# Cross attention of a perceiver block: value tiles taken in three blocks per pair, and the 65 left-over context positions spread over the four row quadrants

## The chip, the cores and the metric

The kernel runs on one core of a Trainium2 chip. The metric is the device time of one execution in microseconds; before and after are compared by the median of several runs.

## The reference, cut to what matters

Thirty-two sequences of 64 positions (width 512) pass through a cross attention to a context of 1601 positions each, then a causal self attention, then a mixture of experts. The change touches the cross attention alone:

```python
def _L0_xattn_ref(input_seq, condition_seq, Wq, bq, Wk, bk, Wv, bv):
    q = jnp.einsum('bsd,ed->bse', input_seq, Wq) + bq
    k = jnp.einsum('btd,ed->bte', condition_seq, Wk) + bk
    v = jnp.einsum('btd,ed->bte', condition_seq, Wv) + bv
    scores = jnp.einsum('bse,bte->bst', q, k)
    attn = jax.nn.softmax(scores, axis=-1)
    attended = jnp.einsum('bst,bte->bse', attn, v)
    return attended

x = x + _L0_xattn_ref(_layernorm(x, axis=-1), ctx_1024, ...)   # ctx: (32, 1601, 512)
```

All of it is float32. The kernel folds the key weights into the queries and applies the value weights after the attention, so that the context itself serves as keys and as values.

## The kernel before, in words

`prepare` (L155) computes the folded queries of all sequences and stores them to the tensor `q_n`, and loads the first context pieces. `cross` (L404) is the cross attention. Then come `self_attention` (L622) and `mixture`, which the change leaves alone.

`cross` works on 16 pairs of sequences. The two sequences of a pair sit in the two column halves of the TensorE array (64 columns each). A sequence's 1601 context positions are 12 full tiles of 128 positions and one rest of 65 (`FULL` = 12, `REST` = 65, `TILES` = 13). They lie in SBUF in slots: the first slot of a pair holds tiles 0 to 6, the second tiles 7 to 11 and the rest (index 5 of the slot, partitions 0 to 64). There are five slots (`SLOTS`), so a pair and a half is in flight beyond the one that is read.

For one pair the score part has 32 steps (`STEPS_S`), 16 on each slot. A step is one transpose on VectorE (`blocks`, L470 to L477: 32x32 blocks of 32 context columns into the ring `z` of 8 entries) and eight matmuls on TensorE (`score`, L554 to L566): one for each row quadrant of 32 rows and each column half. Row quadrant `tb` takes the positions that lie in partitions 32 tb to 32 tb + 31 of each tile. The widths are in `WIDTH` (L416): each quadrant streams 224 columns in the first 16 steps; in the last 16, quadrants 0 and 1 stream 192 columns (five full tiles and 32 of the rest), quadrant 2 streams 161 and quadrant 3 streams 160.

Then VectorE takes the maxima (`greatest`, L479), ScalarE the exponentials (L533 to L536, in five `PIECES`, each with a running sum), TensorE turns the probabilities (`transpose_prob`, L568, 13 transposes in four groups, each copied out by ScalarE, L544 and L547), and TensorE multiplies them by the values (`attend`, L579 to L589: one call for a tile, with two matmuls of 128 rows by 64 columns and 512 streamed columns). The result is scaled, turned (`transpose_attended`, L591) and stored. Each float32 matmul of `score` and `attend` stands in the profile as two matmul records and two weight loads, so a score step has 16 matmul records and an `attend` has 4.

These parts are interleaved by hand in the TensorE stream (L599 to L619), which is unrolled over all pairs: while pair p is scored, the probabilities of pair p-1 are turned ahead of steps 0, 1, 3 and 5, seven value tiles are taken one at a time ahead of steps 9, 12, 15, 18, 21, 24 and 27, and the other six after step 31. The exponentials of pair p read the score banks, so step 0 of pair p+1 waits for them (L602); the six last tiles run meanwhile.

SyncE (L434 to L464) stores results, loads queries and loads the next context pieces: the first slot of a pair is reloaded when seven value tiles are done (`s_pv`, L451), the second when all thirteen are (L454). ScalarE's copy of a turned result (L525) waits for the store two pairs earlier.

Of the kernel before, what the change touches and what calls it, by code (L numbers as in the profile page):

```python
# [38 lines left out]
D1, F1 = 32, 64  # L39
FULL = CTX // P  # L40
REST = CTX - FULL * P
TILES = FULL + 1
MASKED = -3.0e38


def apart(e, spare):


    e.sem_inc(spare[e.engine], 1)


def tile_rows(j):
    return P if j < FULL else REST


def program(nc, a, out):
# [98 lines left out]
def prepare(nc, sem, area, ps, a, ident, qa, qbias, halves, slots, qs, s_c, s_qs, s_qd):  # L155
# [23 lines left out]
    with nc.Block() as block:  # L179
# [44 lines left out]
        @block.vector  # L224
        def _(vec):
            S.start(vec, "dve")

            def normalise(i, u):
                n = i * 2 + u
                vec.wait_ge(s_x[u], i * 16 + 16)  # L230
                layer_norm_stats(vec, stats, mv, xt[u], S, "stat", "mv", n)
                past(vec, "rstd", n + 1)
                past(vec, "mv", n + 1)
                past(vec, "t", n - 1)
                for par in range(2):
                    vec.tensor_scalar(xn[u][:, par * D:(par + 1) * D], xt[u][:, par * D:(par + 1) * D],
                                      mv[:, par, 0:1], rstd[:, par:par + 1], ALU.subtract, ALU.mult)\
                       .then_inc(S["xn"], 1)

            def row_biases(n):  # L240
                past(vec, "r", n + 1)
                vec.tensor_tensor(qbias[:, bass.ds(n * 2, 2)], ps[:, RB, 16:18],
                                  cols[:, 2 * DC:2 * DC + 1].to_broadcast([P, 2]), ALU.add).then_inc(S["re"], 1)
            vec.memset(slots[slot_of(1)][64:P, :, 5, :], 0.0).then_inc(S["pad"], 1)
            normalise(0, 0)
            vec.wait_ge(s_b, 32)
            for c in range(DC):
                vec.tensor_copy(bq_wide[:, c, :], bqc[:, c:c + 1].to_broadcast([P, P])).then_inc(S["wide"], 1)
            for m in range(DC):
                past(vec, "fuse", m + 1)  # L250
                vec.tensor_copy(wqk[:, m, :], ps[:, m, :]).then_inc(S["fused"], 1)
            past(vec, "col", 1)
            vec.tensor_copy(cols, ps[:, RB, 0:2 * DC + 1]).then_inc(S["cold"], 1)
            past(vec, "cold", 1)
            normalise(0, 1)
            with vec.Fori(0, QUADS // 2 - 1) as i:
                for u in range(2):
                    row_biases(i * 2 + u)
                    normalise(i + 1, u)
            for u in range(2):  # L260
                row_biases(QUADS - 2 + u)
# [91 lines left out]
def slot_of(k):  # L353
    return (k + 3) % SLOTS


def context_landed(k):

    return sum(32 if j % 2 == 0 else 64 for j in range(k % SLOTS, k + 1, SLOTS))


def load_context(sp, a, slots, s_c, k, seqs=(0, 1)):

    pair, g = divmod(k, 2)
    u = slot_of(k)
    for b in seqs:
        seq = pair * 2 + b
        main = a["ctx"][seq, 0:FULL * P, :].rearrange("(p j) d -> p j d", j=FULL)
        if g == 0:
            sp.dma_start(slots[u][:, b, 0:7, :], main[:, 0:7, :]).then_inc(s_c[u], 16)  # L370
        else:
            sp.dma_start(slots[u][:, b, 0:5, :], main[:, 7:FULL, :]).then_inc(s_c[u], 16)
            sp.dma_start(slots[u][0:REST, b, 5, :], a["ctx"][seq, FULL * P:CTX, :]).then_inc(s_c[u], 16)


def load_queries(sp, a, qs, s_qs, p):
# [27 lines left out]
def cross(nc, sem, zone, ps, a, ident, qbias, slots, qs, s_c, s_qs, s_qd, early):  # L404
# [5 lines left out]
    probt = zone(TILES, P)  # L410
    att = zone(D)
    att_t = zone(DC, P)
    mx, sums = zone(4), zone(5)
    top, bias = zone(1), zone(1)
    total, recip = zone(1), zone(1)
    WIDTH = (416, 416, 385, 384)  # L416
    PIECES = ((0, 0, TILES, 32), (1, 0, TILES, 32), (2, 0, FULL, 32), (3, 0, FULL, 32), (2, FULL, TILES, 1))
    EXPS = len(PIECES)
    TB, OB, AB = 4, 6, 7

    s_pad = sem("cr_pad")
# [10 lines left out]
    with nc.Block() as block:  # L432
# [33 lines left out]
        @block.vector  # L466
        def _(vec):
            def blocks(p, n):
                g, db = divmod(n, 16)
                k, at = 2 * p + g, STEPS_S * p + n  # L470
                nt = GTILES[g]
                if db == 0:
                    vec.wait_ge(s_c[slot_of(k)], context_landed(k))
                if at >= RING:
                    vec.wait_ge(s_s, at - RING + 1)
                vec.transpose(z[:, at % RING, :, 0:nt * 32].rearrange("p b (j t) -> p b j t", t=32),  # L476
                              slots[slot_of(k)][:, :, 0:nt, db * 32:(db + 1) * 32]).then_inc(s_z, 1)  # L477

            def greatest(p):  # L479
                vec.wait_ge(s_s, STEPS_S * (p + 1))  # L480
                for tb in range(4):
                    vec.reduce_max(mx[:, tb:tb + 1], ps[:, tb, 0:WIDTH[tb]], AX.X).then_inc(s_mx, 1)
                vec.wait_ge(s_mx, 4 * p + 4)
                vec.tensor_reduce(top, mx, AX.X, ALU.max, negate=True).then_inc(s_top, 1)
                vec.wait_ge(s_top, p + 1)
                if p:
                    vec.wait_ge(s_exp, EXPS * p)
                vec.tensor_scalar(bias, top, qbias[:, p:p + 1], qbias[:, p:p + 1],  # L488
                                  ALU.subtract, ALU.add).then_inc(s_bias, 1)

            def denominator(p):
                vec.wait_ge(s_exp, EXPS * (p + 1))
                vec.reduce_sum(total, sums, AX.X).then_inc(s_tot, 1)
                vec.wait_ge(s_tot, p + 1)
                if p:
                    vec.wait_ge(s_att, p)
                vec.reciprocal(recip, total).then_inc(s_rec, 1)

            vec.memset(slots[slot_of(3)][64:P, :, 5, :], 0.0).then_inc(s_pad, 1)
            vec.wait_ge(s_qd, 64 * 16)  # L500
            vec.memset(prob[:, FULL, 2, :], 0.0).then_inc(s_pad, 1)
            for p in range(PAIRS):
                for n in range(STEPS_S):
                    blocks(p, n)
                    if p and n == 1:
                        greatest(p - 1)
                    if p and n == 12:
                        denominator(p - 1)
            greatest(PAIRS - 1)
            denominator(PAIRS - 1)  # L510

        @block.scalar
        def _(act):
# [14 lines left out]
            for p in range(PAIRS):  # L528
                act.wait_ge(s_bias, p + 1)
                if p:  # L530
                    act.wait_ge(s_tot, p)
                    act.wait_ge(s_pt, 4 * p)
                for n, (tb, j0, j1, w) in enumerate(PIECES):  # L533
                    act.activation(prob[:, j0:j1, tb, 0:w],  # L534
                                   ps[:, tb, j0 * 32:(j1 - 1) * 32 + w].rearrange("p (j t) -> p j t", t=w), ACT.Exp,
                                   bias=bias[:, 0:1], accum_out=sums[:, n:n + 1]).then_inc(s_exp, 1)  # L536
                if p:
                    attended(p - 1)
                for g in range(4):
                    act.wait_ge(s_pt, 4 * p + g + 1)  # L540
                    if p and g == 0:
                        act.wait_ge(s_pv, TILES * p)
                    if g < 3:
                        act.copy(probt[:, 4 * g:4 * g + 4, :], ps[:, TB + g % 2, :].rearrange("p (j n) -> p j n", j=4))\  # L544
                           .then_inc(s_pte, 1)
                    else:
                        act.copy(probt[0:96, FULL, :], ps[0:96, TB + 1, 0:P]).then_inc(s_pte, 1)  # L547
                if p:
                    attended_out(p - 1)
            attended(PAIRS - 1)  # L550
# [3 lines left out]
        def _(pe):  # L554
# [13 lines left out]
            def transpose_prob(p, g):  # L568
# [3 lines left out]
                if n >= 2:  # L572
                    pe.wait_ge(s_pte, n - 1)
                for j in quarter(g):
                    tbs, at = (4, (j - 4 * g) * P) if j < FULL else (3, 0)
                    last = pe.transpose(ps[0:tbs * 32, TB + g % 2, at:at + P], prob[:, j, 0:tbs, :].rearrange("p b t -> p (b t)"), ident)
                last.then_inc(s_pt, 1)

            def attend(p, j):  # L579
                if j % 4 == 0:  # L580
                    pe.wait_ge(s_pte, 4 * p + j // 4 + 1)
                if j == 0 and p:
                    pe.wait_ge(s_att, p)
                r = tile_rows(j)
                slot, jj = (slots[slot_of(2 * p)], j) if j < 7 else (slots[slot_of(2 * p + 1)], j - 7)
                for b in range(2):
                    last = pe.matmul(ps[b * SEQ:(b + 1) * SEQ, OB, :], probt[0:r, j, b * SEQ:(b + 1) * SEQ],  # L587
                                     slot[0:r, b, jj, :], start=j == 0, stop=j == TILES - 1)
                last.then_inc(s_pv, 1)  # L589

            def transpose_attended(p):  # L591
# [7 lines left out]
            for p in range(PAIRS):  # L599
# [3 lines left out]
                for n in range(STEPS_S):  # L603
                    if p and n in (0, 1, 3, 5):
                        transpose_prob(p - 1, (0, 1, 3, 5).index(n))
                    if p >= 2 and n == 6:
                        transpose_attended(p - 2)
                    if p and n >= 9 and (n - 9) % 3 == 0 and (n - 9) // 3 < 7:
                        attend(p - 1, (n - 9) // 3)
                    score(p, n)  # L610
                if p:
                    for j in range(7, TILES):
                        attend(p - 1, j)
            for g in range(4):
                transpose_prob(PAIRS - 1, g)
# [1222 lines left out]
```

## Time and profile before

| what | value |
|---|---|
| median of 3 runs | 1514.75 us (1506.93 to 1524.37) |
| profiled execution, its own time | 1523.18 us |
| profiled execution, its span | 1521.4 us |
| mean granted TensorE clock | 0.935 of full speed |
| TensorE busy | 1350.5 us, 89% |
| VectorE busy | 823.1 us, 54% |
| ScalarE busy | 438.3 us, 29% |
| cross attention, first score step to last transpose | about 134.7 to 639 us of the span |

The rows below and the durations come from the profiled execution; its own time is 1.8 us above its span (what lies around the span) and 8.4 us above the median of the runs.

### The profile page before, as it was taken

What the parts mean: (1) busy time and instruction counts of PE and PEld (TensorE: products, weight loads), DVE (VectorE), ACT (ScalarE), POOL (GpSimd) and SP (SyncE); (2) the same over time, 40 slices, a digit from 0 to 9 for tenths busy, and PEclk for the clock granted to TensorE, in tenths of its full rate; (3) what the DMA queues carried; (4) which work ended last, traced back from release to release, by engine and by line L of the source; (5) the groups of instructions that cost most, each with busy time, mean ns of one, the idle gap of its engine ahead of it and who ended that gap; (6) DMA issues with size and microseconds to landing.
All of it is one profiled execution on the core that took longest, in us unless ns stands there. A gap on an engine that the chain in (4) does not pass through costs nothing.

```text
span 1521.4 us, 70167 instructions
## 1 busy us (share of the span) xinstructions
PE 1350.5 (89%) x32072; PEld 932.3 (61%) x32072; DVE 823.1 (54%) x1519; ACT 438.3 (29%) x879; POOL 208.2 (14%) x361
## 2 busy tenths in 40 slices
PE   7896799999999999889999999967888988798896
PEld 4895444444544454356666666646777876687785
DVE  1224566666665665145566555633647465347656
ACT  0230121112211221111122222203636455336544
POOL 0000000000000000001111111102424424023212
PEclk9798899999999999999999999968999999959968
DMA  5476187867886789251100111130203012532202
GB/s 194 143 219 217 38 281 273 269 210 278 300 254 213 279 291 285 72 106 56 51 28 31 55 55 42 56 84 30 111 28 139 38 73 105 222 146 87 107 28 83
DMA packets 57228, 211.96 MB, mean 139 GB/s; under 512 B 11760, under 2 KB 28144, under 8 KB 42640
## 3 DMA queue, kind: packets, MB, share of 16 engines
q1 hardware_dynamic: 57104, 210.14, 40.5%
q8 instruction: 98, 1.61, 0.4%
q14 instruction: 26, 0.21, 0.0%
HBM read 172.37 MB, written 37.75 MB: 138 GB/s over the span
## 4 chain that ended last, share of the span: by engine, by line
PE 42%; DVE 6%; issue 5%; ACT 2%; POOL 2%; DMA 1%; SPq 0%; DVEq 0%; POOLq 0%; ACTq 0%
PE ps L895 8%; PE ps L1675 5%; PE ps L1629 4%; PE ps L886 4%; PE ps L996 4%; PE ps L1644 3%; PE ps L1661 2%; PE ps L1718 2%; PE ps L1600 2%; PE ps L916 2%; PE ps L1701 2%; PE ps L1591 1%; PE ps L906 1%; DMA arena<-h_n 1%; PE ps L938 1%
## 5 line engine op out<-in xcount | busy, mean ns | idle before, releaser
L476 DVE STREAM_TRANSPOSE arena<-arena 128x384 f32<-128x384 f32 (+1 forms) x512 | 275.6, 586 | 133.2 <-PE ps L563 132.7
L563 PE MATMUL ps<-arena 32*64 32x224 f32 (+3 forms) x8192 | 241.3, 348 | 30.3 <-issue 22.0
L563 PEld LDWEIGHTS ps<-arena 32*64 32x64 f32 x8192 | 160.6, 134 | 140.9 <-DVE arena L476 85.8
L587 PE MATMUL ps<-arena 128*64 128x512 f32 (+1 forms) x832 | 207.1, 609 | 0.6 <-issue 0.6
L895 PE MATMUL ps<-arena 128*128 128x256 f32 x512 | 116.3, 386 | 6.2 <-ACT arena L847 6.2
L1515 ACT COPY arena<-ps 128x512 f32<-128x512 f32 x128 | 75.1, 587 | 149.8 <-PE ps L1644 79.4
L895 PEld LDWEIGHTS ps<-arena 128*128 128x128 f32 x512 | 97.1, 192 | 21.7 <-ACT arena L847 7.2
L534 ACT ACTIVATE arena<-ps,arena 128x416 f32<-128x416 f32 (+2 forms) x80 | 41.1, 530 | 229.1 <-DVE arena L488 229.1
L587 PEld LDWEIGHTS ps<-arena 128*64 128x64 f32 (+1 forms) x832 | 49.3, 136 | 86.7 <-issue 86.7
L1675 PE MATMUL ps<-arena 64*64 64x32 f32 x4096 | 91.6, 245 | 10.6 <-DVE arena L1352 5.7
L1675 PEld LDWEIGHTS ps<-arena 64*64 64x64 f32 x4096 | 85.8, 164 | 16.0 <-issue 12.5
L1335 DVE SCALAR_TENSOR_TENSOR arena<-ps,arena 128x512 f32<-128x512 f32 x64 | 68.7, 1104 | 42.6 <-PE ps L1661 42.3
L1629 PE MATMUL ps<-arena 64*32 64x128 f32 x4096 | 71.1, 277 | 14.9 <-issue 6.5
L1629 PEld LDWEIGHTS ps<-arena 64*32 64x32 f32 x4096 | 59.5, 107 | 26.5 <-issue 22.9
L721 POOL MEMSET arena<- 128x128 f32 x1 | 0.2, 205 | 537.3 <-POOLq L432 537.3
L886 PE MATMUL ps<-arena 128*128 128x512 f32 x128 | 61.7, 618 | 8.2 <-ACT arena L876 4.8
L1701 PE MATMUL ps<-arena 64*64 64x256 f32 x1024 | 63.4, 401 | 6.0 <-DVE arena L1345 3.5
L1644 PE MATMUL ps<-arena 32*32 32x64 f32 x4096 | 56.7, 232 | 13.0 <-issue 5.9
L1214 POOL COPY arena<-arena 128x512 f32<-128x512 f32 x64 | 42.3, 666 | 176.9 <-ACT arena L1527 94.0
L799 DVE SCALAR_TENSOR_TENSOR arena<-ps,arena 128x512 f32<-128x512 f32 x32 | 20.6, 686 | 74.1 <-PE ps L906 74.1
L1644 PEld LDWEIGHTS ps<-arena 32*32 32x32 f32 x4096 | 47.7, 108 | 21.1 <-issue 20.6
L313 PE MATMUL ps<-arena 128*128 128x256 f32 x256 | 59.5, 391 | 0.0
(135 smaller groups left out, 1879.0 us busy)
## 6 DMA issues: line engine op xcount, KB each, us to landing
arena<-ctx SPq DMA_DIRECT2D x32, 1792.0 KB
arena<-ctx SPq DMA_DIRECT2D x32, 1280.0 KB
arena<-q_n SPq DMA_DIRECT2D x64, 256.0 KB, 14.0
h_n<-arena SPq DMA_DIRECT2D x16, 1024.0 KB, 4.4
arena<-h_n SPq DMA_DIRECT2D x16, 1024.0 KB, 9.9
arena<-x SPq DMA_DIRECT2D x16, 512.0 KB, 4.6
x_n<-arena SPq DMA_DIRECT2D x16, 512.0 KB, 3.1
arena<-x_n SPq DMA_DIRECT2D x16, 512.0 KB, 3.9
```

The lines of the kernel that those rows point to most:

```text
L476: vec.transpose(z[:, at % RING, :, 0:nt * 32].rearrange("p b (j t) -> p b j t", t=32), slots[slot_of(k)][:, :, 0:nt, db * 32:(db + 1) * 32 ...
L563: last = pe.matmul(ps[b * SEQ:(b + 1) * SEQ, tb, g * 224:g * 224 + w], qs[p % 2][r, db, b * SEQ:(b + 1) * SEQ], z[r, at % RING, b, 0:w], s ...
L587: last = pe.matmul(ps[b * SEQ:(b + 1) * SEQ, OB, :], probt[0:r, j, b * SEQ:(b + 1) * SEQ], slot[0:r, b, jj, :], start=j == 0, stop=j == TI ...
L886: x = pe.matmul(ps[:, par, :], ats[:, c, par::2], w["xwv"][:, c, :], start=c == 0, stop=c == DC - 1)
L895: last = pe.matmul(ps[:, bank, m % 2 * QROWS:(m % 2 + 1) * QROWS], w[n][:, c, m * P:(m + 1) * P], lnt[:, c, :], start=c == 0, stop=c == DC ...
L996: last = pe.matmul(ps[:, 4 + par, :], aot[:, c, par::2], w["swo"][:, c, :], start=c == 0, stop=c == DC - 1)
L1335: vec.scalar_tensor_tensor(h[:, q, :, at].rearrange("p j g -> p g j"), ps[:, b:b + 2, :].rearrange("p b (g x) -> p (b g) x", x=2 * F1)[:, ...
L1515: act.copy(mid[u].rearrange("p (b x) -> p b x", b=2), ps[:, 2 * u:2 * u + 2, 0:256]).then_inc(s_me, 1)
L1629: last = pe.matmul(ps[c * R:(c + 1) * R, 4 * v + hf, o * P:(o + 1) * P], tab_st[v][r, o, :], x, start=True, stop=True)
L1644: last = pe.matmul(ps[q * R:(q + 1) * R, 2 * u + c // 2, m * F1:(m + 1) * F1], xs[rows_c, m, :], four(st_a[u])[rows_c, m // 2 * 2 + k, m % ...
L1675: last = pe.matmul(ps[k * F1:(k + 1) * F1, 2 * u + t, g * D1:(g + 1) * D1], st_h[u][rows_t, g * F1:(g + 1) * F1], two(st_a[u])[rows_t, k, ...
L1701: last = pe.matmul(ps[t * E:(t + 1) * E, 2 * (g % 4) + hf, o % 2 * 2 * P:(o % 2 + 1) * 2 * P], tab_dn[v][r, o, :], x, start=True, stop=True)
```

## The change

The 65 left-over positions are no longer put into partitions 0 to 64 of the last tile. Sixteen of them go to the start of each of the four row quadrants (partitions 0, 32, 64 and 96), and the 65th to partition 16. So each quadrant streams 176 or 177 columns in the last 16 steps. The load of the rest becomes five transfers for a sequence instead of one. The exponentials become four of 384 columns, one of 4 x 16 columns and one of a single column. The last tile is used with all 128 partitions, the unused ones set to zero beforehand. The value tiles of pair p-1 are taken in blocks of three ahead of steps 11 and 22, and seven after step 31.

```diff
+RQ = REST // 4
-def tile_rows(j):
-    return P if j < FULL else REST
@@ prepare, vector
-            vec.memset(slots[slot_of(1)][64:P, :, 5, :], 0.0).then_inc(S["pad"], 1)
+            vec.memset(slots[slot_of(1)][:, :, 5, :], 0.0).then_inc(S["pad"], 1)
@@ context_landed
-    return sum(32 if j % 2 == 0 else 64 for j in range(k % SLOTS, k + 1, SLOTS))
+    return sum(32 if j % 2 == 0 else 32 * 6 for j in range(k % SLOTS, k + 1, SLOTS))
+
+def rest_of(tb):
+    return ((tb * 32, RQ, FULL * P + tb * RQ),) + (((RQ, 1, CTX - 1),) if tb == 0 else ())
@@ load_context
-            sp.dma_start(slots[u][0:REST, b, 5, :], a["ctx"][seq, FULL * P:CTX, :]).then_inc(s_c[u], 16)
+            for tb in range(4):
+                for row, n, first in rest_of(tb):
+                    sp.dma_start(slots[u][row:row + n, b, 5, :], a["ctx"][seq, first:first + n, :]).then_inc(s_c[u], 16)
@@ cross
-    mx, sums = zone(4), zone(5)
+    mx, sums = zone(4), zone(6)
-    WIDTH = (416, 416, 385, 384)
-    PIECES = ((0, 0, TILES, 32), (1, 0, TILES, 32), (2, 0, FULL, 32), (3, 0, FULL, 32), (2, FULL, TILES, 1))
-    EXPS = len(PIECES)
+    RAT = FULL * 32
+    WIDTH = (RAT + RQ + 1, RAT + RQ, RAT + RQ, RAT + RQ)
+    EXPS = 6
@@ cross, vector
-            vec.memset(slots[slot_of(3)][64:P, :, 5, :], 0.0).then_inc(s_pad, 1)
+            vec.memset(slots[slot_of(3)][:, :, 5, :], 0.0).then_inc(s_pad, 1)
-            vec.memset(prob[:, FULL, 2, :], 0.0).then_inc(s_pad, 1)
+            vec.memset(prob[:, FULL, :, :], 0.0).then_inc(s_pad, 1)
@@ cross, scalar
-                for n, (tb, j0, j1, w) in enumerate(PIECES):
-                    act.activation(prob[:, j0:j1, tb, 0:w],
-                                   ps[:, tb, j0 * 32:(j1 - 1) * 32 + w].rearrange("p (j t) -> p j t", t=w), ACT.Exp,
-                                   bias=bias[:, 0:1], accum_out=sums[:, n:n + 1]).then_inc(s_exp, 1)
+                for tb in range(4):
+                    act.activation(prob[:, 0:FULL, tb, :], ps[:, tb, 0:RAT].rearrange("p (j t) -> p j t", t=32), ACT.Exp,
+                                   bias=bias[:, 0:1], accum_out=sums[:, tb:tb + 1]).then_inc(s_exp, 1)
+                act.activation(prob[:, FULL, :, 0:RQ], ps[:, 0:4, RAT:RAT + RQ], ACT.Exp,
+                               bias=bias[:, 0:1], accum_out=sums[:, 4:5]).then_inc(s_exp, 1)
+                act.activation(prob[:, FULL, 0, RQ:RQ + 1], ps[:, 0, RAT + RQ:RAT + RQ + 1], ACT.Exp,
+                               bias=bias[:, 0:1], accum_out=sums[:, 5:6]).then_inc(s_exp, 1)
-                        act.copy(probt[0:96, FULL, :], ps[0:96, TB + 1, 0:P]).then_inc(s_pte, 1)
+                        act.copy(probt[:, FULL, :], ps[:, TB + 1, 0:P]).then_inc(s_pte, 1)
@@ cross, tensor
-                    tbs, at = (4, (j - 4 * g) * P) if j < FULL else (3, 0)
-                    last = pe.transpose(ps[0:tbs * 32, TB + g % 2, at:at + P], prob[:, j, 0:tbs, :].rearrange("p b t -> p (b t)"), ident)
+                    at = (j - 4 * g) * P
+                    last = pe.transpose(ps[:, TB + g % 2, at:at + P], prob[:, j, :, :].rearrange("p b t -> p (b t)"), ident)
-                    last = pe.matmul(ps[b * SEQ:(b + 1) * SEQ, OB, :], probt[0:r, j, b * SEQ:(b + 1) * SEQ],
-                                     slot[0:r, b, jj, :], start=j == 0, stop=j == TILES - 1)
+                    last = pe.matmul(ps[b * SEQ:(b + 1) * SEQ, OB, :], probt[:, j, b * SEQ:(b + 1) * SEQ],
+                                     slot[:, b, jj, :], start=j == 0, stop=j == TILES - 1)
-                    if p and n >= 9 and (n - 9) % 3 == 0 and (n - 9) // 3 < 7:
-                        attend(p - 1, (n - 9) // 3)
+                    if p and n in (11, 22):
+                        for j in range(3):
+                            attend(p - 1, (0, 3)[n // 22] + j)
-                    for j in range(7, TILES):
+                    for j in range(6, TILES):
                         attend(p - 1, j)
```

## Rows read from the trace of the kernel before

**Rows 1.** The page, busy time of engines and the instruction queue.

```profile
PE 1350.5 (89%) x32072; PEld 932.3 (61%) x32072; DVE 823.1 (54%) x1519; ACT 438.3 (29%) x879; POOL 208.2 (14%) x361
...
q8 instruction: 98, 1.61, 0.4%
```

**Rows 2.** Windows by pair: length, busy PE, PEld, DVE, ACT, POOL; clock, DMA share, GB/s.

```profile
555.72:589.78 34.06, 30.43 (x586) 14.96 (x581) 19.78 (x40) 5.96 (x16) 0.00 (x0) 0.95 0.95 303
589.78:618.45 28.67, 28.38 (x588) 14.21 (x582) 18.50 (x38) 5.96 (x16) 0.00 (x0) 1.00 0.62 220
sum 428.70, PE 407.74 PEld 202.67 DVE 275.67 ACT 83.43 POOL 0.00; mean PE 29.12 PEld 14.48 DVE 19.69 ACT 5.96 POOL 0.00
```

**Rows 3.** Timeline of PE, two stretches of one pair: start, busy, matmul records.

```profile
257.44 0.63 PE L576 MATMUL ps<-arena 128*128 128x128 f32 x4 [0.28 <-ACT arena L534]
258.00 0.63 PE L563 MATMUL ps<-arena 32*64 32x224 f32 x16
258.56 0.66 PE L576 MATMUL ps<-arena 128*128 128x128 f32 x4
259.15 1.01 PE L563 MATMUL ps<-arena 32*64 32x224 f32 x32
260.09 0.66 PE L576 MATMUL ps<-arena 128*128 128x128 f32 x4
...
279.79 1.85 PE L563 MATMUL ps<-arena 32*64 32x192 f32 x80
281.57 5.39 PE L587 MATMUL ps<-arena 128*64 128x512 f32 x24
```

**Rows 4.** Timeline of PE, 332 to 339 us and 418 to 426 us: stalls marked issue.

```profile
332.29 0.77 PE L563 MATMUL ps<-arena 32*64 32x161 f32 x23 [0.24 <-issue]
332.98 1.08 PE L587 MATMUL ps<-arena 128*64 128x512 f32 x4
333.99 1.21 PE L563 MATMUL ps<-arena 32*64 32x192 f32 x48
335.13 1.08 PE L587 MATMUL ps<-arena 128*64 128x512 f32 x4
336.14 1.21 PE L563 MATMUL ps<-arena 32*64 32x192 f32 x48
337.27 0.64 PE L587 MATMUL ps<-arena 128*64 128x512 f32 x1
338.48 1.07 PE L587 MATMUL ps<-arena 128*64 128x512 f32 x3 [0.57 <-issue]
...
418.15 0.59 PE L563 MATMUL ps<-arena 32*64 32x224 f32 x4 [0.23 <-issue]
...
425.44 0.88 PE L563 MATMUL ps<-arena 32*64 32x192 f32 x32 [0.68 <-issue]
```

**Rows 5.** Timeline of PE after its longest stall in the steady pairs.

```profile
580.71 0.71 PE L563 MATMUL ps<-arena 32*64 32x160 f32 x3 [3.24 <-issue]
581.35 1.97 PE L587 MATMUL ps<-arena 128*64 128x512 f32 x4
583.25 1.67 PE L563 MATMUL ps<-arena 32*64 32x192 f32 x48
```

**Rows 6.** Timeline of the SP queue: issue of the context loads.

```profile
279.90 0.35 SPq L372 DMA_DIRECT2D arena<-ctx  x1
...
287.00 0.82 SPq L370 DMA_DIRECT2D arena<-ctx  x2
```

**Rows 7.** Windows of 5 us: columns as in rows 2.

```profile
300.00:305.00 5.00, 3.22 (x96) 1.74 (x88) 2.54 (x5) 0.59 (x1) 0.00 (x0) 1.00 0.73 163
305.00:310.00 5.00, 4.64 (x108) 2.27 (x107) 2.39 (x5) 0.00 (x0) 0.00 (x0) 1.00 0.01 3
```

**Rows 8.** Groups by form, 0 to 600 us: exponentials, and their last piece.

```profile
L534 ACT ACTIVATE arena<-ps,arena 128x384 f32<-128x384 f32 x30 | 17.1, 584 | 0.0
...
L534 ACT ACTIVATE arena<-ps,arena 128x1 f32<-128x1 f32 x15 | 4.1, 272 | 0.0
```

More of the change, by code:

```diff
@@ L583, in attend @@
                     pe.wait_ge(s_att, p)
-                r = tile_rows(j)
                 slot, jj = (slots[slot_of(2 * p)], j) if j < 7 else (slots[slot_of(2 * p + 1)], j - 7)
                 for b in range(2):
-                    last = pe.matmul(ps[b * SEQ:(b + 1) * SEQ, OB, :], probt[0:r, j, b * SEQ:(b + 1) * SEQ],
-                                     slot[0:r, b, jj, :], start=j == 0, stop=j == TILES - 1)
+                    last = pe.matmul(ps[b * SEQ:(b + 1) * SEQ, OB, :], probt[:, j, b * SEQ:(b + 1) * SEQ],
+                                     slot[:, b, jj, :], start=j == 0, stop=j == TILES - 1)
                 last.then_inc(s_pv, 1)
```

## The prediction, made before the changed kernel ran

> **What bounds the kernel now.** I read the page first: TensorE is busy 89% of the span, the next engine 54% [rows 1]. So I looked at the windows by pair, cut where the last six value tiles begin (I call this point T). Between T = 189.75 and T = 618.45 lie 14 pairs in 428.70 us, 30.6 us each, and VectorE is busy 19.7 us and ScalarE 6.0 us of them [rows 2]. The reader is to see that TensorE's order of work sets the pair, with some 10 us to spare on VectorE. The last pair, beside a lighter DMA (share 0.62), takes 28.67 us [rows 2]; the same instructions take 30.6 in the mean. So 428.70 - 14 x 28.67 = 27.3 us, 1.95 a pair, are something other than matmuls.
>
> The timeline of TensorE says what. It stalls with the mark "issue": it waits for no semaphore. From the stall that ends at 332.29 to the one before 338.48 I count 23+4+48+4+48+1 = 128 matmul records; with a weight load each that is 256 instructions, and the second stall falls between two records of one value tile, where nothing new is waited for [rows 4]. The instruction queue moved 98 packets, 1.61 MB, so 16.4 KB each [rows 1]: code comes in equal pieces and TensorE stalls at the seam when the next is late. From seam to seam such a piece took 338.48 - 332.29 = 6.2 us, and 425.44 - 418.15 = 7.3 us [rows 4], both beside a context transfer. That is my price of a code piece beside transfers, 6.2 to 7.3, taken as 6.7. In the pair of 28.67 us TensorE is busy 28.38, so it has no such stall; at its end a value tile, three steps, a value tile and five steps are 136 records in 1.01 + 1.14 + 1.01 + 1.78 = 4.94 us [rows 3, 4], a piece in 4.6. So beside light transfers the price is at most 4.6.
>
> The Trainium skill ("Runtime: NRT & Kernel Launch", Instruction fetch mechanics) says that engines are fed in blocks of 256 instructions, the next being fetched while one executes, and that the cost of a boundary is "mostly hidden". The trace agrees on the 256 and not on the hiding: 0.24, 0.57 and 3.24 us stand open in rows 4 and 5. If the page were right for the new order, the sum would be the first rival's, below.
>
> **The change, part by part.** First, TensorE's work with code in time.
>
> Score steps: one step alone takes 258.56 - 258.00 = 0.56, two take 260.09 - 259.15 = 0.94 [rows 3]. So a step of 224 columns is 0.38 and starting a run costs 0.18. In the second half three steps take 335.13 - 333.99 = 1.14 [rows 4] and five 281.57 - 279.79 = 1.78 [rows 3]: 0.32 a step, again 0.18 to start. The slope between 192 and 224 columns is 0.06/32 = 1.9 ns a column; the four quadrants run beside each other and the widest sets the step. From 192 to 177 that is 15 x 1.9 = 28 ns, 16 steps: -0.45 us a pair (bound from the other side: zero, if something other than width holds the step near 0.32).
>
> Value tiles: a single one takes 333.99 - 332.98 = 1.01 [rows 4]; six in a row 5.39 [rows 3], so each further one (5.39 - 1.01)/5 = 0.876, 0.13 less. Now seven singles and six: 7.07 + 5.39 = 12.46. Afterwards two threes and a seven: 2 x 2.76 + 6.27 = 11.79: -0.67. The runs of score steps that a value tile opens drop from seven to two: 5 x 0.18 = -0.90. The wait of 0.28 for the exponentials at T [rows 3] goes: TensorE arrives 0.88 later. What is late next there? The exponentials: now 416, 416, 384, 384 and 1 columns, afterwards four of 384, one of 64 and one of 1; a piece more is some 0.3 (0.272 for one column, 0.584 for 384 [rows 8]), less two narrower ones, so about +0.25. 0.88 - 0.28 = 0.60 covers it, with 0.35 left. Sum of a pair: -0.45 - 0.67 - 0.90 - 0.28 = -2.3. (Laid end to end: 28.67 becomes 26.4.)
>
> The Trainium skill ("TensorEngine Tiling (Array Packing)", on mode switching) says that changing the tiling mode drains the engine. The 0.18 and 0.13 of the rows are that drain here, 0.31 for a round trip; the sum uses the rows.
>
> What the narrower things cost: the transpose of the last tile and its copy with 128 partitions instead of 96, the values with 128 rows instead of 65: nothing, streamed columns are the same. The two memsets keep their columns a partition, the one on `prob` has 128 columns instead of 32, below 0.2 us, once. VectorE: its transposes keep their size. It has 8 entries of lead; in a run of 11 steps TensorE eats 11 in about 4 us, VectorE makes them at 0.5 to 0.6 each (19.78 us busy for 32 and the maxima [rows 2]), so it makes 7 meanwhile and the lead falls to 4 and is refilled in the 2.76 us of a block. Covered.
>
> SyncE: the second slot's load grows from 4 to 12 issues at about 0.4 us (0.35 in rows 6), +3.2 us. It starts when seven tiles are done, now T - 1.7 (279.90 against 281.57), afterwards T + 1. So issues end near T + 6, just when the next load may start (T + 6.3; now 287.00, T + 5.4). Queued behind are that load, a store and the query loads; the store is not waited for until the next T + 20, the rest not until later pairs. The context itself: 2.8 MB from T + 1 at 303 GB/s, the rate of the pair whose DMA share is 0.95 [rows 2], lands near T + 10.5; TensorE needs it at step 16, near T + 18.6. Covered by 7 us, and if the small transfers cost 3 us more, by 4.
>
> Now the code. A pair has 581 pairs of load and matmul, 4.55 pieces [rows 2]. The transfers of a pair fill 279.9 to about 303.7, 24 us, then the DMA rests (share 0.73 at 300 to 305, 0.01 at 305 to 310) [rows 6, 7]. Check on the order of now: from step 9 on there are 396 records, 3.1 pieces, in 17.2 us, about 5.5 each. The first seam is met in time, the second at 6.7, the third at about 6 (its transfer load ends), the other 1.1 at 5.5: 18.8, a stall of 1.6 against 1.95 found. Afterwards: from T to step 11 there are 221 records in 13.9 us: no stall. From there 360 records, 2.8 pieces, hold only 2.76 + 3.85 + 2.76 + 3.13 = 12.5 us of work, and the transfers, which start 2.7 us later against T, last until T + 25, beside almost all of it. Seam to seam 6.7 and 6, the other 0.8 at 4.5: 16.3. Stall 3.8. So 3.8 - 1.95 = 1.85 of the 2.3 comes back: -0.45 a pair; with 0.5 us less or more of price at each of two seams, +0.5 to -1.4. I take -0.5.
>
> Sum: 13 loaded pairs x -0.5 = -6.5. The pair before T = 189.75 and the last one have light transfers: -2.3 + 0.3 each, -4. The end has one more tile behind the scores, +0.6, and pair 1 waits the +0.25 for the exponentials. Pair 0 has no value tiles and stalls for code: 0. Together -9.6, say -10. Then the clock: after the stall of 3.24 us, the granted clock fell (0.95 in that pair), a value tile took 1.97 instead of 1.08 and three steps 1.67 instead of 1.21 [rows 2, 4, 5]: 1.35 us lost. Stalls of that length become more frequent; two in the 13 pairs: +3. I forecast -7: 1523.2 - 7 = 1516 for the profiled execution, which lies 8.4 above the median of the runs; against that median 1514.75 - 7 = 1508. Its own range is -20 to +7 (the +0.5 and -1.4 of the 13 pairs), 1495 to 1522.
>
> **The rivals.** (a) Code costs what it costs now, 1.95 a pair: 15 x -2.3 + 0.9 = -34, 1481. For it: five switches fewer are certain. Against: the pieces with no value tile in them shrink to 8 x 0.3 = 2.4 to 3 us, and seam to seam 6.2 was already the floor beside transfers.
> (b) Slower: stalls join into one of over 3.2 us in every pair, and the clock falls for a stretch each time. Stretches on pure score steps give up half of their length; with the 3.4 us over which rows 5 are slow, +1.7. If the stalls also eat the whole 2.3 saved, 13 x 1.7 = +22, 1537. It decides once a seam falls early in the run of steps 11 to 21 beside transfers, piece work 3, price 7, stall 4. For it: that arithmetic, in about every second pair. Against: matmuls right after the short stalls of rows 4 keep their durations (a value tile 1.08), and only the one of 3.24 is followed by slow ones [rows 5]; and a slow stretch partly runs in time that the next piece would cost anyway.
> (c) The context arrives late for step 16, since the load starts 2.7 us later and in 12 parts: with 4 us beyond my 7 us of slack, 13 x 4 - 10 = +42, 1557. Little speaks for it.
> (d) The step stays near 0.32 at 177 columns: beside code stalls that hides most of it, -5 instead of -7, within the forecast.
>
> **How the numbers follow.** Forecast with (d) 0.58, (a) 0.24, (b) 0.13, (c) 0.05. About 1% (15 us) is what a measurement of this kernel can tell from no change. Faster by over 1%, below 1499.6: all of (a) and a quarter of the forecast's share, 0.24 + 0.14 = 0.38. Slower by over 1%, above 1529.9: half of (b) and (c), 0.11. Within: 0.51. The range reaches to (a) and half way to (b): 1477 to 1526.
>
> **What would show it.** In the changed profile: value tiles as x12, x12, x28 of 2.8, 2.8 and 6.3 us; runs of 11 steps; pairs near 30 us, not 28; no wait for the exponentials at T; "issue" stalls of 2 to 4 us, 128 records apart, in the runs between the blocks, about doubled in sum; lower clock in several pairs. Pairs of 28 us or less with stalls as now would prove the code step wrong; a wait of VectorE for a context transfer at step 16 would prove the cover wrong; pairs over 31 us with a clock below 0.95 would be (b).

## The result and the profile after

The changed kernel takes 1528.08 us (median of 20 runs, 1520.36 to 1533.9), the kernel before 1516.01 us (20 runs): ratio 1.0083, interval 1.0059 to 1.0106, so 12 us slower. The forecast was 7 us faster and the range ended at 1526: it missed in sign and in range. The profiled execution took 1529.43 us, span 1527.6.

The page of the changed kernel, busy time, instruction queue and costliest groups on TensorE (for [rows 1]):

```profile
PE 1331.6 (87%) x32072; PEld 943.9 (62%) x32072; DVE 818.0 (54%) x1519; ACT 440.8 (29%) x911; POOL 207.6 (14%) x361
...
q8 instruction: 98, 1.61, 0.4%
...
L570 PE MATMUL ps<-arena 32*64 32x224 f32 (+2 forms) x8192 | 228.4, 347 | 55.9 <-issue 47.5
...
L593 PE MATMUL ps<-arena 128*64 128x512 f32 x832 | 201.0, 625 | 1.0 <-issue 1.0
```

TensorE is busy 19 us less and the kernel is slower: the code, in as many packets as before, now comes late more often. Windows by pair, from T to T (columns as in [rows 2]), and in the last line all 14 pairs as one window:

```profile
215.79:252.40 36.61, 30.77 (x584) 16.01 (x582) 19.43 (x40) 6.10 (x18) 0.00 (x0) 0.91 0.63 217
252.40:282.19 29.79, 27.97 (x590) 15.56 (x582) 19.53 (x40) 6.09 (x18) 0.00 (x0) 1.00 0.77 266
...
567.13:604.39 37.26, 30.04 (x583) 15.75 (x581) 19.42 (x40) 6.10 (x18) 0.00 (x0) 0.91 0.83 277
604.39:633.45 29.06, 27.90 (x589) 15.47 (x581) 18.38 (x38) 6.10 (x18) 0.00 (x0) 1.00 0.64 219
...
186.65:633.45 446.80, 401.52 (x8142) 221.72 (x8134) 270.81 (x558) 85.35 (x252) 0.00 (x0) 0.96 0.73 250
```

The mean pair went from 30.6 [rows 2] to 446.80 / 14 = 31.9 us. It is not even: pairs of 29.8 stand beside pairs of 36.6 and 37.3, and these have the lower mean granted clock (0.91 against 1.00). What TensorE waited for in the 14 pairs, first before, then after (total us, times, longest us):

```profile
PE ps L563 <- issue: 16.2, 15, 3.2
PE ps L576 <- ACT arena L534: 4.2, 14, 0.4
```

```profile
PE ps L570 <- issue: 41.5, 26, 5.8
PE ps L602 <- issue: 2.5, 2, 1.3
PE ps L593 <- issue: 1.0, 2, 0.5
```

The wait for the exponentials is gone, as forecast. "issue" grew from 16.8 (with 0.6 at the value tiles) to 45.0. The rest of the loss lies inside the busy time: 407.74 us of it before is 29.1 a pair, where the pair of 28.67 us has 28.38 [rows 2]; 401.52 after is 28.7 a pair, where a pair with its code in time has 26.40 (e4, below). So the same matmul records took 0.7 us a pair longer before and 2.3 after. The timeline of TensorE in the pair of 36.61 us shows where:

```profile
228.41 2.11 PE L570 MATMUL ps<-arena 32*64 32x224 f32 x69 [0.21 <-issue]
230.46 2.80 PE L593 MATMUL ps<-arena 128*64 128x512 f32 x12
233.19 4.34 PE L570 MATMUL ps<-arena 32*64 32x224 f32 x174
243.06 0.74 PE L570 MATMUL ps<-arena 32*64 32x176 f32 x2 [5.53 <-issue]
243.73 5.39 PE L593 MATMUL ps<-arena 128*64 128x512 f32 x12
249.05 3.42 PE L570 MATMUL ps<-arena 32*64 32x177 f32 x160
252.40 1.08 PE L593 MATMUL ps<-arena 128*64 128x512 f32 x4
```

From the stall at 228.41 to the one at 243.06 there are 69 + 12 + 174 = 255 records, two pieces of 128 (one record is missing). The first seam lies 47 records into the run at 233.19. In the single records of the trace the last one before it starts at 234.23 and the next at 234.67; the view counts most of that wait as busy, because a record before it lasts 0.35 us. The piece that starts at 234.67 holds 237.53 - 234.67 = 2.9 us of work, and the next comes at 243.06, 8.4 us after that seam. Then the clock is low: the same block of three takes 5.39 instead of 2.80 us. The SyncE queue of that pair:

```profile
216.91 0.35 SPq L374 DMA_DIRECT2D arena<-ctx  x1
217.31 2.10 SPq L377 DMA_DIRECT2D arena<-ctx  x5
...
222.07 0.82 SPq L372 DMA_DIRECT2D arena<-ctx  x2
222.94 0.63 SPq L441 DMA_DIRECT2D at_n<-arena  x1
223.61 2.02 SPq L382 DMA_DIRECT2D arena<-q_n  x4
```

The transfers start at T + 1.1 (216.91 against T = 215.79), before at T - 1.7 [rows 3, 6]. In the profiled executions the stretch behind the last T (633.45 against 618.45) is 9 us shorter after than before, with the same code; the experiments below show both lengths, 893 to 898 and 903 to 906 us, whatever their edit. So the 14 pairs (+18 us) are read from profiles, the verdicts from the medians.

### The profile page after: what moved, and what is told of

It is laid out like the page before. It is cut to its first block, busy times and chain, and to the rows that moved or that the text cites. A ratio compares the mean times of both kernels' runs of the same rounds, so it can differ in the third digit from the quotient of the medians.

```text
span 1527.6 us, 70327 instructions
## 1 busy us (share of the span) xinstructions
PE 1331.6 (87%) x32072; PEld 943.9 (62%) x32072; DVE 818.0 (54%) x1519; ACT 440.8 (29%) x911; POOL 207.6 (14%) x361
## 3 DMA queue, kind: packets, MB, share of 16 engines
q8 instruction: 98, 1.61, 0.4%
## 4 chain that ended last, share of the span: by engine, by line
PE 41%; DVE 6%; issue 5%; ACT 2%; POOL 2%; DMA 1%; SPq 0%; DVEq 0%; POOLq 0%; ACTq 0%
PE ps L902 8%; PE ps L1682 5%; PE ps L1636 4%; PE ps L893 4%; PE ps L1003 4%; PE ps L1651 3%; PE ps L1668 2%; PE ps L1607 2%; PE ps L923 2%; PE ps L1725 2%; PE ps L1708 2%; PE ps L1598 1%; PE ps L913 1%; DMA arena<-h_n 1%; PE ps L945 1%
## 5 line engine op out<-in xcount | busy, mean ns | idle before, releaser
L480 DVE STREAM_TRANSPOSE arena<-arena 128x384 f32<-128x384 f32 (+1 forms) x512 | 270.2, 582 | 171.2 <-PE ps L570 170.8
L570 PE MATMUL ps<-arena 32*64 32x224 f32 (+2 forms) x8192 | 228.4, 347 | 55.9 <-issue 47.5
L570 PEld LDWEIGHTS ps<-arena 32*64 32x64 f32 x8192 | 171.0, 136 | 106.1 <-issue 94.9
L593 PE MATMUL ps<-arena 128*64 128x512 f32 x832 | 201.0, 625 | 1.0 <-issue 1.0
L593 PEld LDWEIGHTS ps<-arena 128*64 128x64 f32 x832 | 58.3, 142 | 119.6 <-issue 119.6
L538 ACT ACTIVATE arena<-ps,arena 128x384 f32<-128x384 f32 x64 | 36.4, 582 | 216.5 <-DVE arena L492 216.5
L1682 PE MATMUL ps<-arena 64*64 64x32 f32 x4096 | 86.1, 236 | 9.4 <-DVE arena L1359 6.5
L1682 PEld LDWEIGHTS ps<-arena 64*64 64x64 f32 x4096 | 80.5, 154 | 14.8 <-issue 11.9
```

The source lines that it names most:

```text
L570: last = pe.matmul(ps[b * SEQ:(b + 1) * SEQ, tb, g * 224:g * 224 + w], qs[p % 2][r, db, b * SEQ:(b + 1) * SEQ], z[r, at % RING, b, 0:w], s ...
L593: last = pe.matmul(ps[b * SEQ:(b + 1) * SEQ, OB, :], probt[:, j, b * SEQ:(b + 1) * SEQ], slot[:, b, jj, :], start=j == 0, stop=j == TILES - 1)
L1682: last = pe.matmul(ps[k * F1:(k + 1) * F1, 2 * u + t, g * D1:(g + 1) * D1], st_h[u][rows_t, g * F1:(g + 1) * F1], two(st_a[u])[rows_t, k, ...
```

## The experiments

Ratios are to the kernel before. The mean pair is the window of 14 pairs over 14, from one profiled execution. e3, e4, e9, e10 and e15 rest on four runs each, the others on nine or more.

| run | edit | ratio (interval) | mean pair, us |
|---|---|---|---|
| changed kernel | | 1.0083 (1.0059 to 1.0106) | 31.9 |
| e1 | order alone | 1.0077 (1.0045 to 1.0109) | 31.2 |
| e2 | layout alone | 1.0017 (0.9985 to 1.0049) | 30.9 |
| e3 | before, light context loads | 0.9878 (0.9829 to 0.9926) | 29.6 |
| e4 | changed, light context loads | 0.9772 (0.9722 to 0.9823) | 28.0 |
| e5 | changed, runs of 4 KB | 1.0047 (1.0017 to 1.0076) | 31.6 |
| e6 | before, runs of 4 KB | 0.9982 (0.9945 to 1.0020) | 30.6 |
| e7 | changed, runs halved | 1.0054 (1.0023 to 1.0084) | 31.7 |
| e8 | changed, order 4, 3, 6 | 0.9915 (0.9876 to 0.9954) | 30.1 |
| e9 | before, late release | 1.0160 (1.0104 to 1.0215) | 32.2 |
| e10 | changed, light query loads | 0.9840 (0.9785 to 0.9895) | 29.4 |
| e11 | changed, queries first | 0.9991 (0.9955 to 1.0027) | 30.7 |
| e12 | e8, queries between | 1.0022 (0.9991 to 1.0053) | 31.5 |
| e13 | e8, late release | 1.0100 (1.0063 to 1.0138) | 31.7 |
| e14 | before, order 4, 3, 6 | 0.9972 (0.9941 to 1.0003) | 30.3 |
| e15 | e8, blocks at 9 and 20 | 1.0106 (1.0024 to 1.0189) | 31.6 |

**Which part: e1 and e2.** The kernel before with the changed order, and the changed kernel with the old order:

```diff
-                    if p and n >= 9 and (n - 9) % 3 == 0 and (n - 9) // 3 < 7:
-                        attend(p - 1, (n - 9) // 3)
+                    if p and n in (11, 22):
+                        for j in range(3):
+                            attend(p - 1, (0, 3)[n // 22] + j)
...
-                    for j in range(7, TILES):
+                    for j in range(6, TILES):
```

> The kernel before with only the order of value tiles changed (3, 3 and 7); the left-over positions stay in one tile. Theory (late code): the seams of 256 instructions fall into runs of 11 score steps beside the transfers; stalls marked issue of 4 to 6 us with low clock behind them, some pairs of 34 to 37 us, as in the changed kernel. Ratio to before 1.005 to 1.012, 1524 to 1534 us. Rival (the five small transfers of a sequence are the cost): this kernel has none of them, so it shows only the saving of the switches: about -20 us or more, ratio 0.985 to 0.99.

> The changed kernel with the value tiles back in the old order (seven single ones, then six). Theory (late code): pieces of code are as long in work as before, so stalls are as before; the narrower steps save up to 0.45 us a pair, part of it hidden: 0 to -7 us, ratio 0.995 to 1.000. Rival (the small transfers cost): slower than before by some 12 us, ratio 1.008.

The order alone makes the loss; it also moves the release of the first slot behind T (in e1 the load starts at 280.69, T = 279.57), and the next experiments part the two. The layout alone cannot be told from no change. It stands just above the 0.995 to 1.000 that I expected and below the rival's 1.008; whether its eight more transfers a pair take back what its narrower steps give was not tried.

**Is it the transfers: e3 and e4.** In `load_context`, for k from 10 on, one tile of each group is loaded, so that the kernel computes on older context (the edit of the first group; the second is cut alike, with 5 in place of 7):

```diff
-            sp.dma_start(slots[u][:, b, 0:7, :], main[:, 0:7, :]).then_inc(s_c[u], 16)
+            w = 7 if k < 2 * SLOTS else 1
+            sp.dma_start(slots[u][:, b, 0:w, :], main[:, 0:w, :]).then_inc(s_c[u], 16)
```

> The kernel before with the context loads from the tenth slot on cut to one tile of seven or five (the rest of the slot keeps older context, so the result is of other data; all instructions of the engines stay). Theory (late code beside transfers): from pair 5 on no stalls marked issue and pairs of 28.7 us: about 10 pairs x 2 us, -18 to -25 us. Rival (stalls have nothing to do with the transfers): no change.

> The changed kernel with the same cut of the context loads. Theory: pairs of 26.4 us from pair 5 on, no low clock there: against the changed kernel -50 to -60 us, against e3 -20 to -25 us, ratio to before 0.970 to 0.978. Rival (the new order is slower by itself, by its switches or by VectorE's lead): pairs stay over 28.7 us also without transfers, and this kernel is not faster than e3.

A pair in the middle of e3, then three of e4 (windows as above):

```profile
422.77:451.42 28.65, 28.37 (x587) 14.23 (x582) 19.67 (x40) 5.95 (x16) 0.00 (x0) 1.00 0.35 96
```

```profile
353.18:379.58 26.40, 26.40 (x590) 15.10 (x582) 19.19 (x40) 6.09 (x18) 0.00 (x0) 1.00 0.39 102
379.58:405.98 26.40, 26.40 (x590) 15.11 (x582) 19.19 (x40) 6.09 (x18) 0.00 (x0) 1.00 0.40 103
405.98:432.38 26.40, 26.40 (x590) 15.11 (x582) 19.20 (x40) 6.09 (x18) 0.00 (x0) 1.00 0.39 103
```

28.65 and 26.40: with the transfers light, TensorE has no "issue" stall in these pairs, and the change saves 2.25 us a pair, as worked out. Not every light pair is like that. Three of e4 took 27.1 to 27.4, with one stall of some 0.5 us each, and one of e3 took 30.64 beside a DMA share of 0.34:

```profile
408.49 0.59 PE L565 MATMUL ps<-arena 32*64 32x224 f32 x4 [1.41 <-issue]
```

So light transfers remove most of the late code, not all; why that piece was late is open. e3 lies at the edge of what was expected (-18 us for -18 to -25). e4's ratio lies in its range; against e3 it gained 19.4 us, just short of the 20 to 25.

**Is it the size of the queued pieces: e5, e6, e7.** Loads of two tiles each (e7: of four and three, three and two); shown is the first group:

```diff
-            sp.dma_start(slots[u][:, b, 0:7, :], main[:, 0:7, :]).then_inc(s_c[u], 16)
+            for j in range(0, 7, 2):
+                w = min(2, 7 - j)
+                sp.dma_start(slots[u][:, b, j:j + w, :], main[:, j:j + w, :]).then_inc(s_c[u], 16)
```

> The changed kernel with each context load cut into transfers of two tiles (4 KB runs instead of 14 and 10 KB), same bytes. Theory (a piece of code waits behind the context pieces already queued on its DMA engine, so its wait goes with their size): code comes sooner, the price of a piece falls from 6.3 to 8.4 us to some 4.5, stalls and low clock mostly go, pairs near 27 us: -40 to -60 us against the changed kernel, 1470 to 1490 us, ratio 0.97 to 0.98. Rival (the code waits for bandwidth, whatever the size of the pieces): no change against the changed kernel, ratio 1.008; or slower, if smaller pieces move less.

> The kernel before with the same cut of the context loads. Theory: its 1.95 us of stalls a pair mostly go, pairs near 28.9 us: -20 to -27 us, ratio 0.982 to 0.987, so e5 beats it by 20 to 35 us. Rival (bandwidth): ratio 1.000.

> The changed kernel with the context loads cut once (4 and 3 tiles, 3 and 2 tiles: runs of 8 to 4 KB). Theory (wait goes with size): between the changed kernel and e5, ratio 0.985 to 0.995. Rival (the number of transfers in flight counts, not their size): no better than the changed kernel.

This theory falls. e5 kept "issue" waits as long as the changed kernel:

```profile
PE ps L574 <- issue: 43.4, 25, 5.0
```

Its ratio, 1.0047, is at most some tenths of a per cent better than 1.0083, the intervals overlap, and e6 is level with before. e7, expected at 0.985 to 0.995, took 1.0054. How finely the context is cut is not what makes the code late.

**Is it the start of the transfers: e8, e9, e13.** In e8 the tiles come as four, three and six, so the seventh is done, and the first slot released, before T (the load starts at 244.36, T = 247.43). In e9 the order is the old one and only SyncE waits longer; e13 does that to e8 (with `+ 8`):

```diff
-                        for j in range(3):
-                            attend(p - 1, (0, 3)[n // 22] + j)
+                        for j in ((0, 1, 2, 3), (4, 5, 6))[n // 22]:
+                            attend(p - 1, j)
...
-                    for j in range(6, TILES):
+                    for j in range(7, TILES):
...
-                    sp.wait_ge(s_pv, TILES * p + 7)
+                    sp.wait_ge(s_pv, TILES * p + 9)
```

> The changed kernel with four tiles ahead of step 11, three ahead of step 22 and six at the end, loads whole: the first slot is released 3 us before T instead of 1 us after it, so the transfers and with them the worst of the code waits lie 4 us earlier against TensorE's work. Theory: the run of steps 11 to 21 is still without a value tile, so pieces are still short in work; the long wait (request 17 to 18 us after the transfers start) moves from T + 19 to T + 14.5, where a piece holds the first block; a part of the loss goes: -3 to -12 us against the changed kernel, ratio 1.000 to 1.006. Rival (the place of the transfers is of no account, only the grouping): ratio 1.008.

> The kernel before, all orders and layouts as they were, but SyncE releases the reload of the first slot two value tiles later (nine instead of seven), so the transfers of a pair start near T + 2 instead of T - 1.7, as late as in the changed kernel. Theory (the start of the transfers decides where the long waits for code fall): the worst wait moves to the last steps before T, where two runs of three and five steps have few value tiles: +5 to +12 us, ratio 1.003 to 1.008. Rival (the grouping into blocks alone makes the loss): ratio 1.000 to 1.002.

> The order 4, 3 and 6 of e8 (0.9915), but SyncE releases the reload of the first slot one value tile later (eight instead of seven). Since the eighth tile comes only after step 31, the transfers start near T + 2 instead of T - 3.5. Theory (the start of the transfers against TensorE's order makes the loss, grouping does not): the gain of e8 is lost and more, about the changed kernel, ratio 1.005 to 1.015, seams of over 8 us near T + 18. Rival (the split 4, 3, 6 is itself the better one): 0.990 to 0.995.

The 14 pairs of e8, of e9 and of e13 as one window each:

```profile
183.42:604.81 421.39, 390.37 (x8142) 218.87 (x8134) 270.00 (x558) 85.45 (x252) 0.00 (x0) 0.98 0.79 266
```

```profile
184.83:635.59 450.76, 422.34 (x8140) 208.48 (x8135) 276.77 (x558) 83.16 (x224) 0.00 (x0) 0.97 0.72 248
```

```profile
183.87:627.85 443.98, 397.93 (x8143) 222.11 (x8135) 270.95 (x558) 85.23 (x252) 0.00 (x0) 0.96 0.74 253
```

e8 gains 1.7% on the changed kernel, some 25 us where I expected 3 to 12. The wait for the exponentials is back in it (5.8 us over the 14 pairs), since six tiles run at T again. e9 changes nothing in TensorE's instructions and loses 1.6%, twice the change's loss and twice the upper end of what I expected. Its "issue" waits in the 14 pairs grew from 16.8 to 24.5 us, its busy time from 407.74 to 422.34: two thirds of its loss lie inside the busy time. e13 takes e8, the best version of this study (0.9915, faster than both kernels), and by one number in one wait turns it into 1.0100, inside its range (its load starts at 249.46, T = 248.34, so 1.1 us behind T as in the changed kernel). The timeline of e9 at the end of a pair, whose transfers began at 251.03 on SyncE, with T = 249.05:

```profile
274.05 0.56 PE L563 MATMUL ps<-arena 32*64 32x192 f32 x11
276.16 1.03 PE L563 MATMUL ps<-arena 32*64 32x161 f32 x37 [1.55 <-issue]
277.12 1.94 PE L587 MATMUL ps<-arena 128*64 128x512 f32 x4
279.00 2.62 PE L563 MATMUL ps<-arena 32*64 32x192 f32 x80
281.55 5.38 PE L587 MATMUL ps<-arena 128*64 128x512 f32 x24
```

The open stall of 1.55 us is followed by slow matmuls there: a value tile of 1.94 instead of 1.08, and five steps in 2.55 instead of 1.78; the mean granted clock of that pair is 0.95. A part of e9's loss may be another: VectorE waited 2.4 us in all for context; how much of that reached TensorE was not read.

**What in the transfers: e10, e11, e12.** The query loads cut to a sixteenth (e10), or moved: ahead of the context loads (e11, its added lines shown), between them in e8's order (e12).

```diff
+                if p + 3 < PAIRS:
+                    sp.wait_ge(s_s, STEPS_S * (p + 2))
+                    load_queries(sp, a, qs, s_qs, p + 3)
                 if 2 * p + 5 < 2 * PAIRS:
```

> The changed kernel with the query loads from the third pair on cut to a sixteenth (the result is of wrong queries; all engine instructions stay). If the query loads make the peak of the wait for code (5.4 us near T + 18, when the context is nearly through and they follow): the peak goes, waits of 3 to 4 us stay, -20 to -35 us against the changed kernel, ratio 0.985 to 0.995. If the context transfers alone make it: only the shorter burst shows, -3 to -10 us, ratio 1.002 to 1.006.

> The changed kernel with the query loads issued at T, ahead of the context loads, instead of 7 us later behind them. Same bytes, same burst of 24 us, started 1 us earlier. If the query loads make the peak: it moves to T + 1 to T + 8, where a piece of code holds the block of seven and work for 8 us: -15 to -30 us against the changed kernel. If only the amount queued counts: -2 to -6 us.

> The order 4, 3 and 6 of e8 with the query loads issued between the two context loads of a pair. e8 took 0.9915 of before. If the query loads make the peak: 0.980 to 0.988; if only the amount queued counts: 0.990 to 0.993.

e10 gains 2.4% on the changed kernel, a little more than the first case asked; but it also ends the burst earlier, so it does not part kind from amount. e11 has the same bytes and wins back 0.9%, 14 us: more than the amount would give (2 to 6), just under the other case (15 to 30). e12 fits neither (0.980 to 0.988 or 0.990 to 0.993): it lost 1.1% against e8. Its waits on TensorE, from a profiled execution that was the slowest of its ten, 12.5 us above their median:

```profile
PE ps L573 <- issue: 25.7, 15, 2.9
PE ps L605 <- issue: 7.3, 2, 4.0
```

L605 is the transpose of the attended rows at step 6: there two stalls, 7.3 us together, stand that e8 did not have. So the worst of the wait may follow the query loads to an earlier place. e11, whose longest stall is 3.6 us instead of 5.8, agrees with that. It is not shown: here two stalls of one execution carry it. Why these loads (8 KB for each of 32 partitions) should hold code back more than the context does was not tried and stays open.

**The layout in the better order, and the blocks two steps earlier: e14, e15.**

```diff
-                    if p and n in (11, 22):
-                        for j in ((0, 1, 2, 3), (4, 5, 6))[n // 22]:
+                    if p and n in (9, 20):
+                        for j in ((0, 1, 2, 3), (4, 5, 6))[n // 20]:
```

> The kernel before with only the order 4, 3 and 6; the left-over positions stay in one tile and one transfer. Theory: order and early release make the gain of e8; the layout adds a few us at most: ratio 0.990 to 0.997. Rival (the narrower steps of the layout carry the gain): 0.998 to 1.003.

> e8 with its blocks ahead of steps 9 and 20 instead of 11 and 22, so the release comes two steps (0.6 us) earlier still and the last run of steps is 12 long. Theory: the start of the transfers at T - 4; the run of 12 steps at the end has the light part of the DMA behind it: ratio 0.986 to 0.994. Rival (the length of the run decides): slower than e8, 0.995 to 1.003.

e14 cannot be told from no change (its interval reaches 1.0003), and its interval overlaps e8's: the 0.6% between them, which would be the layout's share, is likely and not certain. In the old order (e2) the layout brought nothing that can be measured.

Now grouping and release can be parted. In the layout of before, with the transfers starting ahead of T, the single tiles took 1 and the blocks 0.9972 (e14); with the start behind T the single tiles took 1.0160 (e9) and the blocks 1.0077 (e1). In the changed layout, ahead of T, 1.0017 (e2) and 0.9915 (e8); behind T the blocks took 1.0083 and 1.0100 (the changed kernel and e13). Where both were run, the blocks are no worse than the single tiles at the same start, and a late start costs 1.0 to 1.9%. So the loss comes with the late release, not with the grouping. Two things are not quite equal in this: with an early start the blocks are 4, 3 and 6, with a late one 3, 3 and 7 but for e13, and the single tiles with a late start were run in the layout of before alone.

e15 was meant as a small step on and lost 1.9% against e8; at 1.0106 it lies above its range and above its rival's, and I expected neither. Its timeline:

```profile
296.30 2.80 PE L593 MATMUL ps<-arena 128*64 128x512 f32 x12
300.75 2.65 PE L570 MATMUL ps<-arena 32*64 32x177 f32 x128 [1.65 <-issue]
306.67 2.46 PE L570 MATMUL ps<-arena 32*64 32x177 f32 x64 [3.27 <-issue]
309.06 6.02 PE L593 MATMUL ps<-arena 128*64 128x512 f32 x24
```

In its last run of twelve steps (192 records) lies a whole piece, 128 records, of 2.65 us of work, and the next came 306.67 - 300.75 = 5.92 us after it: 3.27 open. The transfers of the next pair had started at 299.14, as this run began. My theory said the DMA was light there, and this order made it not so. That is how this loss may come about; in e8 they also start as the last run begins, and why two steps more cost so much was not tried.

## Why the prediction was wrong

**The bound** was read right: TensorE's own work, and code that comes late in pieces of 256 instructions beside transfers. e3 and e4 show both, and in e4's pairs of 26.40 us, all of them TensorE's busy time, nothing else holds a pair. One reading was wrong: "27.3 us, 1.95 a pair, are something other than matmuls". Of these 27.3 only 16.8 are open "issue" stalls; some 10 lie in matmul records that took longer, as the mean of 29.12 against 28.38 in its own rows says [rows 2].

**TensorE's work** was right to 0.05 us: 28.67 to 26.4 was forecast, 28.65 to 26.40 measured with light transfers. A run of ten narrow steps took 3.18 us, so 0.30 each beside the 0.18 to start (0.29 was forecast), the blocks 2.80 (less the overlap: 2.73 from start to start) and 6.24, the wait for the exponentials went. VectorE's lead and the context for step 16 were covered too: TensorE waited for neither.

**The step that failed is the one on SyncE.** "It starts when seven tiles are done, now T - 1.7, afterwards T + 1 ... Covered": I asked of the later start only whether the context still arrives in time. It does. What it moved is the stretch in which code is slow. e9 makes that one move in the kernel before and loses 1.6%; e13 makes it in e8 and loses more than e8 had gained. In the code step I did let the transfers last to T + 25, but kept one price. What this step let through stands in two terms of the sum, the code and the clock.

**The sum of the 14 pairs.** Against pairs with their code in time (14 x 28.65 before, 14 x 26.40 after) the kernel before lost 27.6 us and the changed one 77.2. So the work fell by 31.5 us and the losses grew by 49.6: 28.2 in open "issue" stalls (16.8 to 45.0) and 21.4 inside the busy time (10.8 to 32.2).

**The price of a code piece**, "6.2 to 7.3, taken as 6.7", was two rows of one kind of place. After the change the piece asked for near T + 19, at the end of the transfers, came after 8.4 us with 2.9 us of work to cover it. I wrote 3.8 us lost a pair instead of 1.95; 31.9 - 26.4 = 5.5 was measured instead of 1.95, with the clock.

**The clock** was priced at two falls of 1.35 us, +3 in all. Seven of the 14 pairs stand at 0.90 to 0.95, one did before; behind the stall of 5.53 one block of three alone lost 2.6 us. What the clock cost has a bound: the missing share of each pair's clock times its length adds up to 17 us after and 1.7 before. So of the growth of 49.6 us at most 15 are the clock's and at least 34 the code's, where I had +3 and 13 x 1.85 = +24. Both terms were too small, and the clock's, if it took its bound, by the larger part: the code alone would then have left the pair near +0.2, inside the +0.5 to -1.4 that I gave. How the growth divides between the two below that bound is not shown.

**The rivals.** (b), slower by joined stalls and clock, is in the main what happened, at 1528 instead of 1537, with 0.13 of the chance. Its condition, "once a seam falls early in the run of steps 11 to 21 beside transfers, piece work 3, price 7, stall 4", is met in the pair shown with 2.9, 8.4 and 5.53. It asked for such a stall in every pair; four of the 14 pairs have one of over 4 us, and these took over 34 us. (a) is e4's case and needs transfers that are not there. (c) did not occur.

Beside light transfers the rule of the Trainium skill ("Runtime: NRT & Kernel Launch", Instruction fetch mechanics), boundaries "mostly hidden", agrees with most pairs of e3 and e4, and the stall of 1.41 us in e3 does not fit it; beside the full ones the 5.53 above speaks against it.

## What to carry to other kernels

An unrolled TensorE stream is itself a transfer (98 packets, 1.61 MB here): look for "issue" stalls a fixed number of instructions apart, and weigh each stretch of cheap instructions (many of them, little work) against what DMA is doing in that stretch. Batching that removes switches also thins some pieces of code, and whatever moves the release of a buffer moves the burst of transfers that the code has to pass. Here the changed layout in the order 4, 3, 6 with an early release was 0.85% faster than before, and the same with a late one 1.0% slower, so the two have to be tuned together.

## What the runs showed that I had not expected

The number in one wait on SyncE was worth 1.6% (e9, nine for seven) and 1.9% (e13 against e8, eight for seven) with every engine's work unchanged. A piece of code took 4.6 us or less in most pairs beside light transfers, and 8.4 us at the end of a burst. Cutting context transfers from 14 KB to 4 KB a run left the time the same within 0.4% (e5, e6). And TensorE's matmuls are slow behind the stall of 1.55 us in e9, where in the kernel before they kept their time behind one of 2.15 (the value tile takes its 1.08), so the length of one stall does not tell it:

```profile
305.36 0.49 PE L563 MATMUL ps<-arena 32*64 32x160 f32 x4 [2.15 <-issue]
305.78 1.08 PE L587 MATMUL ps<-arena 128*64 128x512 f32 x4
```
